# Steps without MLP work in another order: scores between the input products, the next rows turned and modulated in mid-step, SyncE issuing all first maxima

## The reference, cut to what matters

```
layer 0, 1, 3:  mod = cond @ W_ada + b         (shift, scale, gate, twice; layers 1 and 3: silu(cond))
                h  = LN(x) * (1 + scale) + shift
                q, k, v = h @ Wqkv + b         (16 heads of 16; layer 1 causal)
                x += gate * (softmax(q k^T / 4) v @ Wo + bo)
                x += gate2 * (gelu(mod2(LN(x)) @ W1 + b1) @ W2 + b2)
layer 2:        h  = gamma(cond) * LN(x) + beta(cond)
                h1 = (softmax(q k^T) / 16) v @ Wp + bp + x
                x  = gamma * LN(h1) + beta + h1          (no MLP)
```

## Time and profile before

| | us |
|---|---|
| median of 3 runs (lowest, highest) | 1169.93 (1163.79, 1175.97) |
| the profiled execution | 1166.1 |
| its span, first to last instruction | 1164.3 |
| TensorE busy | 1072.6 (92%) |
| VectorE busy | 836.8 (72%) |
| ScalarE busy | 570.4 (49%) |
| GpSimd busy | 324.4 (28%) |

### The profile page before, as it was taken

The page is one execution under the profiler, slowest core; times in us unless marked ns, Lnnn a source line. Parts: engine busy times, 40 slices in busy tenths (PEclk is TensorE's granted clock), DMA queues, the critical chain, the costliest instruction groups (busy, mean ns, idle before and its releaser), DMA issues.

```text
span 1164.3 us, 22743 instructions
## 1 busy us (share of the span) xinstructions
PE 1072.6 (92%) x8002; PEld 870.3 (75%) x8002; DVE 836.8 (72%) x2187; ACT 570.4 (49%) x1140; POOL 324.4 (28%) x408
## 2 busy tenths in 40 slices
PE   5799999999998999999999988888888999999987
PEld 4568888888886888888888755555566888788776
DVE  4467777777777878778777666666677777777743
ACT  4235654645653455445456434444445456555451
POOL 3033321333325433213333011111134333113332
PEclk9689999999999999999999999999999999999999
DMA  6723333223342235322233433333352134322300
GB/s 232 244 78 100 110 111 93 67 61 109 110 156 98 79 110 166 110 88 74 69 106 117 137 111 108 111 111 100 102 185 87 54 115 119 120 82 72 110 3 19
DMA packets 103279, 123.26 MB, mean 106 GB/s; under 512 B 9040, under 2 KB 96080, under 8 KB 102288
## 3 DMA queue, kind: packets, MB, share of 16 engines
q1 hardware_dynamic: 102608, 121.73, 33.7%
q10 hardware_dynamic: 576, 0.30, 0.1%
HBM read 85.16 MB, written 35.78 MB: 104 GB/s over the span
## 4 chain that ended last, share of the span: by engine, by line
PE 52%; DVE 13%; issue 11%; DMA 9%; ACT 5%; SPq 4%; POOL 4%; ACTq 1%; POOLq 0%; DVEq 0%
PE dense L1253 9%; PE dense L1181 7%; PE o_banks L1331 7%; PE s_bank L1278 6%; PE st_bank L1315 5%; DMA k_stack<-qk_dram 4%; PE o_banks L1210 4%; PE dense L1236 4%; DMA q_stack<-max_t 4%; DVE neg_max L865 3%; POOL hid_lo L522 3%; SPq L366 3%; PE o_banks L1160 2%; ACT probs L673 2%; PE o_banks L1339 2%
## 5 line engine op out<-in xcount | busy, mean ns | idle before, releaser
L673 ACT ACTIVATE probs<-st_bank 128x512 f32<-128x512 f32 (+1 forms) x512 | 264.6, 571 | 167.2 <-PE st_bank L1315 115.6
L865 DVE TENSOR_REDUCE neg_max<-s_bank 128x2 f32<-128x512 f32 x384 | 255.1, 684 | 52.4 <-PE s_bank L1278 48.9
L1278 PE MATMUL s_bank<-k_stack,q_stack 96*128 96x256 f32 (+1 forms) x1024 | 227.9, 314 | 22.0 <-DMA k_stack<-qk_dram 10.4
L1278 PEld LDWEIGHTS s_bank<-k_stack,q_stack 96*128 96x128 f32 x1024 | 166.5, 194 | 64.4 <-DVE neg_max L865 23.0
L522 POOL TENSOR_TENSOR hid_lo<-hid,hid_hi 128x512 fp32r<-128x512 f32 x96 | 125.7, 1320 | 267.4 <-DVE hid_hi L977 267.4
L474 POOL TENSOR_TENSOR veps<-mv,eps_c 128x2 f32<-128x2 f32 x65 | 16.5, 253 | 511.5 <-DVE mv L831 511.5
L1315 PE MATMUL st_bank<-q_stack,k_stack 98*128 98x512 f32 x384 | 148.9, 456 | 10.4 <-DMA q_stack<-max_t 8.2
L661 ACT ACTIVATE hid<-dense,vec 128x256 f32<-128x256 f32 x192 | 80.5, 471 | 110.5 <-PE dense L1236 110.5
L1181 PE MATMUL dense<-ht,w_sb 128*128 128x256 f32 x512 | 130.6, 396 | 3.8 <-ACT ht L612 1.3
L1331 PE MATMUL o_banks<-probs,v_aug 128*32 128x256 f32 (+1 forms) x2048 | 124.5, 386 | 10.1 <-DVE xg L904 5.8
L1236 PE MATMUL dense<-ht,w_hi 128*128 128x256 f32 x384 | 116.4, 303 | 7.3 <-DVE ht_lo L970 6.1
(11 more groups left out here) (136 smaller groups left out, 1886.9 us busy)
## 6 DMA issues: line engine op xcount, KB each, us to landing
q_stack<-qk_dram SPq DMA_DIRECT2D x192, 128.0 KB, 2.9
k_stack<-qk_dram SPq DMA_DIRECT2D x96, 256.0 KB, 4.1
par_sb<-par_dram SPq DMA_DIRECT2D x32, 512.0 KB, 5.3
qk_dram<-q_hi SPq DMA_DIRECT2D x32, 256.0 KB, 2.1
qk_dram<-q_lo SPq DMA_DIRECT2D x32, 256.0 KB, 2.2
qk_dram<-k_hi SPq DMA_DIRECT2D x32, 256.0 KB, 2.2
qk_dram<-k_lo SPq DMA_DIRECT2D x32, 256.0 KB, 2.1
w_sb<-w SPq DMA_DIRECT2D x5, 1024.0 KB, 7.3
```

The lines of the kernel that those rows point to most:

```text
L673: nc.scalar.activation(probs[p % 4][:, kt, :, q0:N], src, ACT.Exp, scale=SCORE_SCALE[l]).then_inc(p_sb, 1)
L865: nc.vector.tensor_reduce(neg_max[:, qt, 2 * p:2 * p + 2], split3(bank[:]), AX.X, ALU.max, negate=True).then_inc(s_max, 1)
L1278: ins = mm(bank[:, e * N:e * N + k1], q_stack[g.par][0:KB, 2 * p + e, qt * P:(qt + 1) * P].bitcast(F32R), k_stack[g.par][0:KB, p, 0:k1].bi ...
```

## The change

The `else` branches of all five programs are rewritten; steps with MLP work keep theirs.

- TensorE puts single score tiles between the q, k and v products (before: q and k in one piece, then pairs of tiles). `score_t(g, 3)` comes before the projection. `ht1_early(n)` turns the next rows but one into `dense[1]` ahead of `values(g, 0)`; `ht1_t(n)` at the end of the step goes away. `max_turn(a, 0)` stands ahead of `ao_turn(g)`, and tiles 4 to 7 of a come one place earlier.
- ScalarE: `modulate1(n)` runs in mid-step, ahead of `out_copy(g, 0)`; the first exponentials stand between `q_hi`, `k_hi` and the copy of v. It no longer sends the first rows of maxima.
- VectorE: tiles 10 and 11 ahead of `q_lo`, 12 and 13 ahead of `k_lo`. The norm of n moves from between the tiles of a to the middle of the step, around `max_copy(g, 1)`, and with it GpSimd's `power(n)` and `pick(n)`. `max_split(a, 0)` comes ahead of `out_norm(g, 1)`.
- SyncE issues the first rows of every step, at the end of the step before; those of step 0 after the first loads.

```diff
@@ sync: step, and ahead of run_steps
-                if a.exists and HAS_MLP[g.layer]:
+                if a.exists:
                     max_rows(sp, a, 0)
...
+            max_rows(sp, Step(0), 0)
             run_steps(sp, step, after)
@@ gpsimd: step
-                if inputs_of(a):
+                mlp = has_mlp(g)
+                if inputs_of(a) and not inputs_ready(g):
                     pool.wait_ge(mod_cols, 2 * (a.layer + 1))
...
+                if not mlp and n.exists:
+                    power(n, 0, ln1_mv, ln1_veps, ln1_rstd)
+                    wait(pool, ht1_sb, n.count(1, 0))
+                    pool.wait_ge(mod_cols, 2 * (n.layer + 1))
+                    pick(n, 0, mod1_now)
@@ scalar: step, the branch without MLP
+                    query_hi(a)
+                    exps(g, 0)
+                    key_hi(a)
+                    exps(g, 1)
+                    value_copy(a)
+                    exps(g, 2, 3)
                     max_rows(act, g, 1)
+                    modulate1(n, dense[1])
                     out_copy(g, 0)
-                exps(g, 4, 5, 6, 7)
-                if not mlp:
+                    exps(g, 4, 5, 6, 7)
                     out_copy(g, 1)
@@ vector: step, the branch without MLP
-                    if inputs:
-                        query_lo(a)
-                        key_lo(a)
-                    maxima(g, 10, 11, 12, 13, 14, 15)
+                    maxima(g, 10, 11)
+                    query_lo(a)
+                    maxima(g, 12, 13)
+                    key_lo(a)
+                    maxima(g, 14, 15)
                     max_split(g, 1)
+                    ln1_a(n)
                     max_copy(g, 1)
+                    wait(dve, ln1_stats, n.count(1, 1))
+                    norm_mv(0, ln1_mv)
                     if c.exists:
                         first_residual(c)
+                    ln1_c(n)
...
-                    maxima(a, 6)
+                    maxima(a, 0, 1, 2, 3, 4, 5, 6, 7)
+                    max_split(a, 0)
                     out_norm(g, 1)
                     if modulated:
                         modulation_cols(modulated)
-                    maxima(a, 7)
-                    max_split(a, 0)
                     max_copy(a, 0)
@@ tensor
+            def ht1_early(n):
+                wait(pe, xn1_done, n.count(1, 1))
+                wait(pe, k_lo_sb, n.count(1, 0))
+                transposed(dense[1], xn1, ht1_ps)
```

More of the change, by code:

```diff
@@ L260, in inputs_of, with has_mlp, inputs_ready @@
             return a.exists and (a.reg is not None or a.off > 0)
+        def has_mlp(g):
+            c = g.back(1)
+            return c.exists and HAS_MLP[c.layer]
+        def inputs_ready(g):
+            return g.off > 0 and not has_mlp(g.back(1))
         def modulation_of(g):
@@ L531, in step @@
                     pick(a, 0, mod1_now)
-                mlp = c.exists and HAS_MLP[c.layer]
                 if g.reg is None and g.off == 0:
@@ L544, in step @@
                     hidden_lo(c, 0, 1, 2)
-                if n.exists:
+                if mlp and n.exists:
                     power(n, 0, ln1_mv, ln1_veps, ln1_rstd)
@@ L613, in modulate, with modulate1 @@
                 ins.then_inc(done, 1)
-            def modulate1(a):
+            def modulate1(a, bank):
                 wait(act, v_ps, a.count(1, 0))
                 wait(act, mod1_now, a.count(1, 1))
-                modulate(a, 0, o_bank[1], ht1_ps, a.count(1, 1), ht1, ht1_sb)
+                modulate(a, 0, bank, ht1_ps, a.count(1, 1), ht1, ht1_sb)
             def modulate2(c):
@@ L676, in step @@
             def step(g):
-                c, a = g.back(1), g.ahead(1)
-                inputs, mlp = inputs_of(a), c.exists and HAS_MLP[c.layer]
-                if inputs:
-                    modulate1(a)
+                c, a, n = g.back(1), g.ahead(1), g.ahead(2)
+                inputs, mlp = inputs_of(a), has_mlp(g)
+                if inputs and not inputs_ready(g):
+                    modulate1(a, o_bank[1])
                 if mlp:
@@ L688, in step @@
                         key_hi(a)
[L689 to L690 removed]
+                    exps(g, 2)
+                    modulate2(c)
+                    exps(g, 3)
                     if inputs:
[L692 to L701 removed]
+                        value_copy(a)
                     bring_table(ACT.Gelu)
@@ L723, in _ @@
             first = Step(0)
-            modulate1(first)
+            modulate1(first, o_bank[1])
             query_hi(first)
@@ L1063, in step @@
                 else:
-                    maxima(a, 0, 1, 2)
-                    if n.exists:
-                        ln1_a(n)
-                        wait(dve, ln1_stats, n.count(1, 1))
-                    maxima(a, 3)
-                    if n.exists:
-                        norm_mv(0, ln1_mv)
-                    maxima(a, 4)
-                    if n.exists:
-                        ln1_c(n)
-                    maxima(a, 5)
-                    maxima(a, 6)
+                    maxima(a, 0, 1, 2, 3, 4, 5, 6, 7)
+                    max_split(a, 0)
                     out_norm(g, 1)
@@ L1425, in step @@
                 else:
-                    if inputs:
-                        q_product(a, 0)
-                        q_product(a, 1)
-                        k_product(a)
+                    q_product(a, 0)
+                    score(g, 10)
+                    q_product(a, 1)
+                    score(g, 11)
                     score_t(g, 0)
-                    score(g, 10, 11)
-                    if inputs:
-                        v_product(a, 0)
+                    k_product(a)
+                    score(g, 12)
                     score_t(g, 1)
-                    score(g, 12, 13)
-                    if inputs:
-                        v_product(a, 1)
-                    score(g, 14, 15)
+                    v_product(a, 0)
+                    score(g, 13)
+                    v_product(a, 1)
+                    score(g, 14)
                     score_t(g, 2)
+                    score(g, 15)
+                    score_t(g, 3)
                     if c.exists:
@@ L1442, in step @@
                     max_turn(g, 1)
-                    score_t(g, 3)
                     if c.exists:
@@ L1448, in step @@
                         modulation_cols(modulated, part=0, parts=4)
+                    ht1_early(n)
                     values(g, 0)
@@ L1459, in step @@
                     score_t(g, 6)
-                    score(a, 4)
+                    score(a, 4, 5)
                     score_t(g, 7)
-                    score(a, 5)
+                    score(a, 6)
                     if modulated:
@@ L1465, in step @@
                     values(g, 1)
-                    score(a, 6)
+                    score(a, 7)
                     out_turn(g, 1)
-                    score(a, 7)
+                    max_turn(a, 0)
                     ao_turn(g)
-                    if n.exists:
-                        ht1_t(n)
-                    max_turn(a, 0)
                     if modulated:
```

17 lines of the change are left out of this document (3 added, 14 removed).

## The result

| | us |
|---|---|
| before, median of 4 runs beside it | 1168.14 |
| after, median of 4 runs (lowest, highest) | 1181.89 (1179.77, 1186.4) |
| ratio, 95% interval | 1.0121 [1.0081, 1.0161] |
| profiled execution after (before) | 1179.77 (1166.1) |
| its span after (before) | 1178.0 (1164.3) |

The change makes the kernel 1.2% slower. The forecast was 1167, in a range of 1153 to 1179: wrong, and outside the range.

The account below looks back on a forecast made before the run. No engine is full; a chain of waits through all of them sets the 29 us step. +1.0 - 1.7 - 1.0 + 0 = -1.7 on 1166.1 gives 1164.4, 1168.2 in medians' terms; forecast 1167, range 1153 to 1179.

Parts of the forecast that it names:

- the second half of the steady step: From tile 0's start to the step's end: 9.68 us before, 0.3 off and 0.25 on, so 9.65.
- rival C: Clock falls after two new TensorE idle stretches in each of steps 17 to 24: +19, sum 1184; chance 0.14.
- the gap ahead of the turn: TensorE idle 2.2 us at mid-step, ahead of `ht1_early`, until `xn` is done; the turn at +15.2.
- station (c): Mid-step stacks: traffic ends 9.2 us behind `k_lo`, 10.3 + 9.2 = +19.5, where tile 0 starts; before at +19.31.
- rival B: k part doesn't bind and the lower clock goes: steady step 28.3 us, whole 1153; chance 0.25.
- The test that I set for C: If steps 17 to 24 show a clock under 0.9, the slower case of 1184 holds.
- The walk through the first half: Steady step: first transposed pair at +4.55 after 1.25 us idle, `k_lo` ends at +10.3, 2.1 later than before.
- Who issues the rows: SyncE instead of ScalarE sends the first rows: same 4.2 us from copy to TensorE in a steady step.
- The sign that I read from the earlier trace: Rows of the chain: 4.30 against 3.82 us, agreeing in sign with rows standing behind loads in ring order.
- Steps 17 and 18, -1.7: Condition's rows begin earlier, so q in step 18 waits until about +4.4; of 3.6 us extra 1.9 left: -1.7 us.
- Steps 0 and 1, -1.0: End of step 0: split ahead of the condition's columns, -1.5; late k in step 0 loses perhaps 0.5: -1.0 us.
- Step 24, 0 with bounds -1 and +6: Weight loads go out behind rows, `ht1_early` 1.1 us late; counted 0, upper bound if spills queue behind weights.

Follow-up runs that it names:

- k_product_first: Changed kernel with the k product, tile 12's scores and `k_hi` ahead of the first transposed pair, and `k_lo` ahead of maxima 12 and 13: 1162.8 us, ratio 0.9975.
- fill: Changed kernel with unread matmuls on TensorE, 14 ahead of the early turn and 9 ahead of tile 0: 1177.51 us, ratio 1.0079.
- fill_second: Changed kernel with only the 9 unread matmuls ahead of tile 0: 1171.45 us, one run.
- fill_first: Changed kernel with only the 14 unread matmuls ahead of the early turn: 1187.36 us, one run.
- before_fill: Kernel before with unread matmuls in three gaps of steps 18 to 24: 1165.49 us, ratio 0.9962.
- par_late: Changed kernel in which SyncE loads the next step's parameters only when the nine stack loads have landed: 1177.28 us, ratio 1.0079.
- k_rest_first: Changed kernel with one VectorE instruction moved, `k_lo` ahead of the maximum of tile 13: 1159.71 us, ratio 0.9899.
- rows_sync_only: Kernel before with one edit of the change, SyncE issues all first rows of maxima: 1175.28 us, ratio 1.0049.
- tuned_par_late: Changed kernel, k product first, `k_lo` behind maximum 12, other reordering, step 24's weight loads issued earlier, parameters loaded after the stacks: 1151.04 us, ratio 0.9837.
- rows_scalar: Changed kernel with the first rows of maxima issued by ScalarE again in steps 0 and 17 to 24: 1180.33 us, ratio 1.0129.

## Why the prediction was wrong

**The step that failed is the second half of the steady step, 9.65 us, taken at the upper clock; and with it the weight of rival C.** The steady step was forecast at 29.15 us, "19.5 + 9.65". The first half held: tile 0 waits for `k_stack<-qk_dram`, and starts at +18.94. The second half takes 11.75 in place of 9.65, with the second `values` at 3.64 in place of 1.93. I had named the mechanism (the clock falls behind a wait) and given it 0.14, and I had looked for it in the wrong place: behind the gap ahead of the turn (2.2 forecast, 1.69 measured) and behind one of 1.25 ahead of the first pair (none). k_product_first keeps the gap of 1.69 and a clock of 1.00. What matters in the steady steps is the wait ahead of tile 0, which my own station (c) had brought to the bound and which I then priced at its length alone. Take steps 19 to 23 of the changed kernel and of those made from it without unread matmuls added: with a wait of at most 0.6 us there the clock stayed at 1.00 in 23 cases of 23; with one of 0.7 or more it fell in 18 of 22. The kernel before was a warning: its steps 18, 21 and 22 fell to the lower level in the second half, though nothing there waits for a stack, and I used this for rival B (the lower clock may go) and too little against the change. (the earlier trace rows is of step 21 and not of step 20, as I had it, and the other step like it is 22.) How long a single gap is doesn't tell these steps apart: ahead of the pair that waits for the second rows, steps 19 and 20 idled 1.02 and 1.07 us and held the clock, 21 and 22 idled 0.57 and 0.92 and didn't. The test that I set for C, a clock under 0.9 in steps 17 to 24, is met with 0.89.

The Trainium skill ("TensorE: Matmul & The Clock Gate", Part 1: The HAM clock gate) has the throttled state as the default, which activity releases. By that rule occupying TensorE with anything should hold the clock. In steps 18 to 23 fill agrees in five, fill_second in four, and fill_first, which occupied TensorE elsewhere, in none. before_fill agrees in sum (0.9962).

**Its size.** Without the dip, step 20 would be 30.69 - 1.71 = 28.98, and par_late's step 23, at a clock of 1.00, is 28.89, with tile 0 at +19.40 and 9.49 behind it: the sum of the forecast was right, but for a step at the upper clock. Of the 16.2 us that steps 17 to 24 lose, 6.5 lie ahead of tile 0, most of it in steps 18, 21 and 23, where the stacks land latest, and in step 24, where the first `values` takes 3.14. The other 9.7 lie behind tile 0. There the second `values` alone has 9.4 of dips against 4.3 before, 5.1 net; the 4.6 that are left weren't taken apart. Against the forecast's terms: steps 19 to 23 were to lose 0.8 in all and lost 10.4; steps 17 and 18 were to win 1.7 and lost 4.8.

**The walk through the first half.** "TensorE idles 1.25 us" ahead of the first pair: it didn't. From the end of the copy to the pair's start were 2.9 us, where I had taken 4.2. So `k_lo` ended at +8.87 and not +10.3. That is an error of 1.4 in my favour, and another of 0.9 took most of it back: I counted the stack as there when its traffic ended, and TensorE starts 0.9 after that. The forecast of 19.5 for tile 0 was near 18.94 by two errors of opposite sign. VectorE idled 0.89 behind `k_hi`, waiting for tile 13, and then did maximum 13 first. That this one maximum with the wait for its scores, 1.42 of `k_lo`'s end, decides (k_rest_first), I had not seen.

**Who issues the rows.** Priced at nothing in a steady step: right (rows_sync_only, 28.5 to 29.7 with no wait at tile 0). The sign that I read from the earlier trace rows has no effect there.

**Steps 17 and 18, -1.7.** q did start at +4.64 in step 18 and not at +6.16, 1.5 gained, and the step is 3.28 longer: the stack, 2.77 of wait, and the clock. Step 17 is 1.5 longer; `k_lo` ends there at +10.50 in place of +8.15. **Steps 0 and 1, -1.0:** -4.6 (the same stretch is 109.1 in par_late and 109.8 in fill_second, so rather -3.6 to -4.6). The place was right, and the size was four times what I had put. The split is ahead of the columns as forecast; q starts at 76.91 where it started at 81.94 before. **Step 24, 0 with bounds -1 and +6:** +1.0. In rows_sync_only the step with the same delay of the spills is 5.6 longer; in the changed kernel the delay lies beside the wait of the early turn for `xn` (3.7, the longest of that wait), and I take it that this is why it costs little more. The turn itself comes 3.0 later than in a steady step, where I had put 1.1. **Steps 2 to 16:** +3.1 that I hadn't counted, in code that didn't change. That stretch varies between kernels whose code there is the same (529.9 before, 533.0 after, 533.5 in k_rest_first, 537.0 in tuned_par_late); from one profile each I can't say whether the change has a part in it.

**What the range missed.** I had worked out rival C's 1184 from the profiled execution, and the profiled execution after took 1179.8; on the scale of the medians C stands near 1187, and the median is 1181.9. It comes that near by luck: C put a fall behind each of two gaps in eight steps, and neither gap is the one; measured was about one fall in a step, behind a third place, and a longer one. With C at 0.3 the range would have taken it in.

**What stays open.** What exactly lowers the clock: par_late's step 23 waits 1.47 at tile 0 and holds it, its step 19 waits 0.97 and doesn't, and k_rest_first's step 17 loses it with no wait there. That `k_lo`'s place costs the steady steps their clock is shown, a rule for the fall is not.

## What to carry to other kernels

When a wait moves to a new place on TensorE, price it twice: its own length, and the work behind it at the lower clock, if the kernel before already dips in some of its steps. When products are interleaved with other work, look for the one whose result starts the longest chain (here `k_lo`: spill, nine loads, tile 0) and put its whole path first on every engine that it passes; one 0.7 us reduction ahead of it, with 0.9 us of waiting for its scores, made the difference between 1.2% slower and 1.0% faster. End a DMA's cost where its reader starts, not where its traffic ends.

## What the runs showed of the hardware

- A stretch at the lower clock gave 3.64 us for 32 matmuls that take 1.93 at the upper one. In the changed kernel it set in behind waits of 1.0 us and more at tile 0. A wait of 1.69 us at the turn 4 to 5 us earlier in the step didn't bring it by itself (k_product_first, k_rest_first: clock 1.00). Waits at tile 0 of 1.47 (par_late, step 23) and 1.53 us (rows_scalar, step 23) didn't either, and in k_rest_first's step 17 it came with none.
- In step 19 of par_late the last traffic of nine loads and the reader's start lie 0.9 us apart.
- Three loads of 256 KB took 3.5 to 4.3 us from their last issue to the reader's start in steps 19 to 23 of par_late, and 3.8 to 5.2 in the changed kernel, where a load of 512 KB follows them by 0.1 to 0.5 us (one execution each).
- Three weight loads, 2.25 MB together, ahead of four spills on one queue (rows_sync_only, step 24): from `k_lo`'s spill to the first load behind it 5.6 us in place of 0.4, and tile 0 waited 5.39 us.
